# Two-layer graph kernel on one core: the row-end work of sweep 2 stands one tile later on ScalarE and VectorE

## What is computed

```python
# layer 0
fc = x @ W0 + b0
d = 1 / (sqrt(adj.sum(1)) + 1e-8)
x1 = layernorm(x + (adj * d[:, None] * d[None, :]) @ fc)
# layer 1
a = adj + eye;  s = 1 / sqrt(a.sum(1))
out = layernorm(x1 + relu((a * s[:, None] * s[None, :]) @ (x1 @ W1) + b1))
```

## Time and profile before

| | |
|---|---|
| median of three runs | 1847.39 us |
| the profiled execution | 1842.48 us, span 1840.7 us |
| TensorE busy | 1647.4 us, mean granted clock 0.967 |
| VectorE, ScalarE, GpSimd busy | 1205.3, 750.7, 161.4 us |
| moved by DMA | 573.38 MB, mean 312 GB/s |

### The profile page before, as it was taken

The page is one execution under the profiler, slowest core; times in us unless marked ns, Lnnn a source line. Parts: engine busy times, 40 slices in busy tenths (PEclk is TensorE's granted clock), DMA queues, the critical chain, the costliest instruction groups (busy, mean ns, idle before and its releaser), DMA issues.

```text
span 1840.7 us, 16886 instructions
## 1 busy us (share of the span) xinstructions
PE 1647.4 (89%) x6136; PEld 1117.6 (61%) x6136; DVE 1205.3 (65%) x1550; ACT 750.7 (41%) x904; POOL 161.4 (9%) x177
## 2 busy tenths in 40 slices
PE   0247889999999999978899999999999999999996
PEld 0123344444444444446777777877877878888885
DVE  1444556776866684347756556464465899999996
ACT  5544333211000000034545434443444777777774
POOL 0000000000000000011100000000000011111111
PEclk9778899999999999989999999999999999999998
DMA  9999999998879766246675665665565999999992
GB/s 387 421 421 421 421 422 408 416 402 343 363 328 367 316 248 262 103 163 237 229 260 218 231 245 199 239 239 206 218 230 206 418 420 410 398 384 389 395 397 83
DMA packets 85906, 573.38 MB, mean 312 GB/s; under 512 B 10400, under 2 KB 10656, under 8 KB 20288
## 3 DMA queue, kind: packets, MB, share of 16 engines
q1 hardware_dynamic: 76320, 541.23, 73.9%
q0 software_dynamic: 9504, 31.07, 4.3%
HBM read 556.79 MB, written 15.47 MB: 311 GB/s over the span
## 4 chain that ended last, share of the span: by engine, by line
PE 73%; DVE 12%; DMA 9%; issue 2%; ACT 1%; POOL 1%; SPq 0%; DVEq 0%; ACTq 0%
PE acc L677 29%; PE acc L701 14%; PE acc L703 14%; PE acc L702 14%; DMA lent<-adj_tiles 5%; DVE low L820 5%; DMA own<-adj_tiles 2%; DMA own<-adj_far 1%; DMA lent<-adj_far 1%; DVE stats L798 1%; DVE run L831 1%; PE turned L613 1%; DVE h L896 1%; PE mixed L644 1%; ACT high L720 1%
## 5 line engine op out<-in xcount | busy, mean ns | idle before, releaser
L701 PE MATMUL acc<-high,feat_high 128*128 128x512 f32 x1336 | 534.0, 400 | 41.4 <-DVE low L820 32.3
L677 PE MATMUL acc<-lent,feat 128*128 128x512 f32 x1168 | 524.2, 608 | 20.8 <-DVE feat L868 14.9
L703 PE MATMUL acc<-high,feat_low 128*128 128x512 f32 x1336 | 525.4, 393 | 0.0
L702 PE MATMUL acc<-low,feat_high 128*128 128x512 f32 x1336 | 524.6, 393 | 0.0
L820 DVE TENSOR_TENSOR low<-own,high 128x1024 fp32r<-128x1024 f32 x330 | 389.0, 1219 | 140.2 <-ACT high L720 137.4
L677 PEld LDWEIGHTS acc<-lent,feat 128*128 128x128 f32 x1168 | 226.4, 195 | 305.7 <-issue 287.9
L720 ACT CAST high<-own 128x1024 fp32r<-128x1024 f32 x330 | 335.2, 1055 | 185.7 <-PE acc L703 148.5
L831 DVE TENSOR_TENSOR run<-run,lent 128x2048 f32<-128x2048 f32 x135 | 309.3, 2291 | 133.9 <-DMA lent<-adj_tiles 128.5
L701 PEld LDWEIGHTS acc<-high,feat_high 128*128 128x128 f32 x1336 | 253.8, 190 | 102.2 <-issue 46.1
L703 PEld LDWEIGHTS acc<-high,feat_low 128*128 128x128 f32 x1336 | 253.4, 190 | 54.9
L702 PEld LDWEIGHTS acc<-low,feat_high 128*128 128x128 f32 x1336 | 254.2, 190 | 50.4
(11 more groups left out here) (69 smaller groups left out, 673.4 us busy)
## 6 DMA issues: line engine op xcount, KB each, us to landing
lent<-adj_tiles SPq DMA_DIRECT2D x237, 1024.0 KB, 12.1
own<-adj_tiles SPq DMA_DIRECT2D x197, 1024.0 KB, 6.2
lent<-adj_far SPq DMA_DIRECT2D x60, 1024.0 KB, 22.3
own<-adj_far SPq DMA_DIRECT2D x18, 1024.0 KB, 23.4
x_in<-x_rows POOLq DMA_DIRECT2D x32, 256.0 KB, 6.5
sums_rows<-stage POOLq DMA_DIRECT2D x27, 256.0 KB, 6.8
sums_in<-sums_rows POOLq DMA_DIRECT2D x27, 256.0 KB, 9.1
x_t<-x_cols SPq DMA_DIRECT2D x16, 256.0 KB, 14.9
```

The source lines that it names most:

```text
L677: mm = nc.tensor.matmul(bank, feat0[:, j * Q + q, :], raw(n)[:, q * T:(q + 1) * T], start=(u == plan.first[g] and q == 0), stop=(u == plan ...
L701: nc.tensor.matmul(bank, f_high, a_high[:, chunk], start=(u == plan.first[g] and q == 0), stop=False)
L702: nc.tensor.matmul(bank, f_high, a_low[:, chunk], start=False, stop=False)
L703: mm = nc.tensor.matmul(bank, f_low, a_high[:, chunk], start=False, stop=(u == plan.last[g] and q == Q - 1))
```

## The change

One number of the table is changed.

```diff
-AHEAD = {1: 0, 2: 0, 3: 1}
+AHEAD = {1: 0, 2: 1, 3: 1}
```

## The result

The changed kernel has a median of 1812.79 us (four runs, 1810.62 to 1815.33), the kernel before beside it 1846.4 us (four runs, 1844.37 to 1847.57). The ratio is 0.982, with a 95% interval of 0.9802 to 0.9837: 33.6 us, or 1.8%, faster. The forecast was 1820 with a range down to 1813. The direction and the mechanism are as forecast, but the gain is 6.3 us over the 27.3 us that the sum gave, and the time came out at the very lower end of the range (1812.79 against 1813).

The account below looks back on a forecast made before the run. TensorE was taken to bound sweep 2. Row ends 18.5, half clock 2.7, row 0 1.0 and opening 5.1 sum to 27.3 us: 1815.2 from the profiled 1842.5, 1820.1 from the median; range 1813 to 1834.

Parts of the forecast that it names:

- What bounds: Sweep 2 is TensorE's; its idle stretches can be won, including 20.0 us of waits for residues after the opening.
- The row ends: Sweep 2, rows 10 to 1: VectorE makes residues before the waiting bank emptying, so TensorE's waits go, 18.5 us.
- the schedule after T: From the bank's freeing by the last heavy take: split +1.0, next residues +1.6, `add_x` to +6.5, following residues ready +7.8.
- Half clock: Two half-clock matmul stretches, in rows 8 and 7, go with their waits: 2.7 us, ends 0 and 2.7.
- The second rival: Slow-clock stretches in sweep 2 move elsewhere instead of vanishing: gain 21.2 us, time 1826, chance 0.17.
- Row 0: Last takes of sweep 2, leading into sweep 3: 0.5 us of 1.5 waiting left; gain 1.0 us, ends 0 and 1.5.
- The opening: Sweep 2's takes 178 to 192: the new order costs and gives, net gain 5.1 us, ends 0 and 7.
- The chain of steps ahead of take 183: Opening: `make_x1` of row 13, split, residues, `add_x`, residues, `make_x1` take 10.0 us, then `features1_low`; take 183 starts at 841.4.
- Nothing: ScalarE's casts of takes 284 and 285, moved ahead of row-end work at row 1's end, were claimed to change nothing.

Follow-up runs that it names:

- vector-only: Only VectorE's row-end work stands one take later in sweep 2, ScalarE's order unchanged, against the kernel before: 1843.3 us, ratio 0.9985.
- scalar-only: Only ScalarE's row-end work stands one take later in sweep 2, VectorE's order unchanged, against the kernel before: 1845.7 us, ratio 0.9997.
- below-190: Both engines' row-end work stands one take later only for takes below 190 (rows 15 to 11), against the kernel before: 1844.1 us, ratio 0.9985.
- bank-only: Only VectorE's emptying of the layer-0 bank stands one take later in sweep 2, against the kernel before: 1847.7 us, ratio 1.0003.
- features-first: As the changed kernel, but the three steps making layer-1 features keep their old place for takes up to 183: 1807.2 us, ratio 0.9786.

## Why the prediction was right, and where its size was off

**What bounds.** Right. TensorE's waits from 890 us on went from 20.0 to 0.3 us, and the stretch is now 508.6 us busy out of 508.9.

**The row ends.** The mechanism and the schedule after T were right to 0.1 us, and the vector-only kernel shows that it is VectorE's order. The term was 18.5 + 2.7, and 1.0 for row 0, together 22.2; it measured 27.3. The heading of the term says rows 10 to 1, but its waits are those of nine rows, 9 to 1: the two of row 10 lie ahead of take 193 and were summed in the opening. The mis-sized step is the price of a wait: I took the idle time that a row states. TensorE's timeline of the kernel before, around the 1.81 us wait of the earlier trace rows, shows the rest (the last matmul ahead of it, and the fourth behind):

```profile
1342.48 0.39 PE L703 MATMUL acc<-high,feat_low 128*128 128x512 f32 x1
...
1345.45 0.40 PE L701 MATMUL acc<-high,feat_high 128*128 128x512 f32 x1
```

Without a wait the next start would be 0.227 after 1342.48, at 1342.71. It was at 1344.68, so 1.97 was lost, not 1.81: the idle time is counted from the modelled end of a matmul, which lies 0.16 behind the point at which the next could have started. The three matmuls from 1344.68 to 1345.45 took 0.77 instead of 0.68. A stop costs 0.25 us over its idle time, and 17 stops went (18 to 1): 4.3 us. With 19.7 of idle time and 2.7 of half clock that makes 26.7 of 27.3; the last 0.6 is not traced. At one row's end it is nearly the same, 0.23 for each stop: from T to take 283 it took 11.19 us before (1336.79 to 1347.98) and takes 8.63 now, 2.56 less, where the two waits were 2.10. The range's lower end didn't provide for this; it held because of allowances made for other reasons, which is luck.

**Half clock.** In the stretch from 193 to 298 the granted clock went from 0.99 to 1.00, so the half-clock stretches went with the waits, as taken. The second rival (they stay) didn't come. How many there are isn't set by the waits. The scalar-only, below-190 and bank-only kernels have nearly the same waits as the kernel before, and in their timelines half-clock matmuls follow the 1.8 us wait at one row end (row 8), at one (row 1) and at three (rows 7, 4 and 2), against two before (rows 8 and 7); the stretch took 535.4, 535.4 and 537.5 us against 536.2. So the 2.7 is what the one profiled execution had, and needn't hold for another. It was also too high by what the slow matmuls save: with them the second wait of 0.3 us is absent, and rows 8 and 7 became 3.5 and 3.6 us shorter, rows 5 to 1 2.6 to 2.7, which is about 1.0 for each half-clock stretch and not 1.3. The Trainium skill ("TensorE: Matmul & The Clock Gate", Part 1) says of the start of a kernel that the number of slow matmuls varies between runs of one kernel. Here it is the places behind equal waits in mid-kernel that vary, between kernels that differ elsewhere, and no run here compares two executions of one kernel. What decides stays open.

**Row 0.** 0.27 us of wait is left where I had 0.5, and nothing was lost in sweep 3: 415.4 us from take 298 to the end in both.

**The opening.** 5.1 forecast, 5.1 measured, and the way there was right in its steps: first take 2.27 later (2.35), take 183 1.9 later (1.8), take 187 1.2 later (0.8), then the waits of row 10 gone but for 0.4 (0.6). That it agrees to the tenth is luck. The prediction's own terms, 0.8 + 5.0 - 0.6, give 5.2; at take 188 the changed kernel was 0.3 ahead instead of 0.8, and from there to take 193 it gained 4.85 instead of 4.4. The chain of steps ahead of take 183 is borne out by the features-first kernel, which shortens it and gets 7.7 us.

**ScalarE.** "Nothing" was right where it was said, in the long rows from take 200 on (the kernel with ScalarE's move below 200 only); at row 9's end, behind a late opening, the move was worth 1.3 us. I had carried it over to the opening in the expectation for the vector-only kernel, and there it was wrong by 26 us.

**The rest.** 32.5 us is what the stretches show; the other 1.1 of the 33.6 between the medians lies within their interval and in sweep 1, which the change doesn't touch.

## What to carry to other kernels

Where several engines work through lists in order, ask of each instruction that waits what stands behind it that could already be done, and walk the list instruction by instruction: the worth of a move is what the last link then says, not the idle time ahead of the moved instruction (8.57 us here, worth nothing alone). Two engines that hand work to each other must be moved together where their row-end work is dense, and the right distance can differ between the dense opening and the long rows. Price a stop of TensorE by distances of starts, and compare two profiles stretch by stretch, behind the parts that vary by themselves.

## What the runs showed of the hardware

- A stop of TensorE between matmuls of 128x512 costs 0.25 us over the idle time that its row states (0.16 ahead, 0.09 behind it, at the wait of 1.81 us ahead of take 282 in the kernel before).
- With the same 1.8 us waits at nine rows' ends, four kernels of this study took 535.4 to 537.5 us for the same stretch. In the kernel before two of the nine waits were followed by nine matmuls at a granted clock of 0.5; in the scalar-only, below-190 and bank-only kernels it was one, one and three.
- Sweep 1, the same program in all profiles, ended between 798.5 and 803.9 us.
